# A two-layer block on one core: local attention with stationary values, the Mamba scan in PSUM, a new plan

## The chip, the cores and the metric

One Trainium2 chip, one of its cores. The metric is the device time of one execution of the whole program in microseconds (us). The engines are named as in the profile: PE is TensorE (PEld its weight loads), DVE is VectorE, ACT is ScalarE, POOL is GpSimd, SP issues most DMAs.

## What is computed

The input is 16 sequences of 256 tokens with 128 features, in fp32. Two blocks follow each other. Block 0 adds to x a Mamba layer (a scan over time with 256 inner channels and 16 states) and a layer of 8 experts of which each token takes one. Block 1 adds an attention over 16 heads with an arc-cosine kernel (called g here) and a two-layer local-attention transformer (called l here). Cut to the parts that the change touches:

```python
# Mamba: per channel d and state n, over time
h = dA * h + dBx                          # dBx = dt * B[n] * xs[d]
y = einsum('bdn,bn->bd', h, c)            # c = C[n]
y = (ys + D * xs) * silu(z)
# local attention: 8 heads of 64, windows of 64, a query sees its own window and the one before
sim = einsum('bhwid,bhwjd->bhwij', bq, bk)
sim = where(mask, -max, sim)              # mask = (i < j) | (i > j + 64)
attn = softmax(sim, axis=-1)
out = einsum('bhwij,bhwjd->bhwid', attn, bv)
x = x + out @ wo
```

## The kernel before, in words

The 16 sequences are taken as 8 pairs of 512 tokens. Everything is fp32 but the masks, which are bf16 and are added to scores by a product with a bf16 identity. Each unit of work ("m_scan", "pt", ...) has a number for the pair or layer, a stream b (which of the two sequences of a pair) and a step k. `all_units` says what each unit comes after and when it is wanted, with the offsets LATER (per kind) and STREAM (per pair). `schedule` then walks through time with the costs in STAGES, gives every engine an order and every unit its PSUM banks (8 in all), and the five programs issue their instructions in that order. The engines meet only at semaphores.

**Mamba** (units m_*). A pair has 16 steps; one step is 2 of the 16 states by one of the two halves c of 128 channels. Steps go state group by state group, both halves of each (`divmod(k, CH)`). m_ex makes dA by two Exp (ACT L1312). m_bx multiplies B by du into the SBUF tile hB (DVE L1530), m_scan scans hB in place (DVE L1536), m_hc multiplies it by C in place (DVE L1542), and m_sum adds hB up over the states by 8 transposes into a PSUM bank (PE L1013), one bank for each half, so two banks are held through the 16 steps. B and C are read from DRAM by SP, 512 KB each and broadcast over the partitions, once for each state group (L1887, L1893), two buffers of each. m_turn copies the sum out (ACT L1318) and transposes it back; m_fin finishes it on DVE.

**Local attention** (per layer, per sequence b: 32 times). heads transposes q and k. Four score units of two heads: on PE the mask (L1140, 128x128 stationary), then the second 128 queries (L1144, four tiles of 64x64) and the first 128 (L1147, two tiles of 64x128); DVE takes the negative maximum (L1684). Four pt units of two heads compute the scores again, transposed: mask (L1155), scores in three pieces for each head (L1159), then the maximum spread over the columns by two fp32 products with identities (L1165, L1166), and ACT takes Exp into the tile PT (L1426); the two buffers of PT are shared by both sequences. Eight pv units, one a head, have PT stationary and the values with a column of ones moving, 65 columns (L1179 to L1181). After three, three and two heads on takes the reciprocal of the ones' column (DVE L1694) and multiplies (DVE L1698). oT transposes the result (8 transposes of 128x128, PE L815, which is the line of all transposes but the sums') and ACT copies it out in two pieces (L1429). wo multiplies by the output weights (L1195), then come layer norm and the feed-forward part.

An fp32 product is two PE instructions in the profile (x2), a transpose is one. L1077 is the product of the g attention: values stationary in 32 columns, four heads in four groups of columns, 256 columns moving.

The lines of POOL that matter are the two additions L1823 and L1827, each of two SBUF tiles.

Of the kernel before, what the change touches and what calls it, by code (L numbers as in the profile page):

```python
# [6 lines left out]
ALU = mybir.AluOpType  # L7
# [3 lines left out]
P = 128  # L11
SEQS, L, DM = 16, 256, 128
NPAIR = SEQS // 2
T = 2 * L
# [4 lines left out]
NG = 2  # L19
# [30 lines left out]
OH = 3  # L50
OG = -(-LH // OH)
# [21 lines left out]
    "g_out": [("PE", 0.89), ("DVE", 0.68)], "out": [("DVE", 0.69), ("SP", 0.1)], "zeros": [("DVE", 0.34)],  # L73
    "shift": [("PE", 0.22), ("ACT", 0.97)], "norm": [("DVE", 0.17), ("ACT", 0.5)], "qn": [("DVE", 1.22)], "heads": [("PE", 0.88), ("ACT", 1.03)],
    "score": [("PE", 1.0), ("DVE", 0.61)], "pt": [("PE", 2.32), ("ACT", 0.7)], "pv": [("PE", 0.64)], "on": [("DVE", 0.78)],
    "oT": [("PE", 0.44), ("ACT", 0.6)], "wo": [("PE", 1.83), ("DVE", 0.42)], "ln": [("PE", 0.69), ("DVE", 0.77), ("ACT", 0.54)],
# [8 lines left out]
DUAL = ("m_du", "m_bx", "m_scan", "m_hc", "m_fin", "qn", "g_hd")  # L85
# [3 lines left out]
         "norm": "ln", "pt": "ln", "ln": "ln", "m_in": "silu", "g_tan": "tan", "gelu": "gelu"}  # L89
SWITCH = 127.0  # L90

LATER = {"down": 9, "e_down": 27, "e_lg": -177, "e_ln": 421, "e_load": -1379, "e_place": 30, "e_pre": -533, "e_route": -824,
         "e_scat": 827, "e_store": -1322, "e_tr": 261, "e_up": 40, "e_xn": -205, "e_xt": -160, "f_ln": 337, "f_tr": -1175,
         "f_xn": 125, "f_yg": 758, "g_av": 86, "g_avT": -766, "g_ev": -1332, "g_hd": -30, "g_ln": 728, "g_norm": -329, "g_oT":
         355, "g_out": 176, "g_pow": 587, "g_qkv": 73, "g_score": 51, "g_sq": 85, "g_sub": 1181, "g_tan": 60, "gelu": -398,
         "heads": 45, "hid": -32, "l_weights": 124, "ln": -103, "ln2": 5, "lnT": -6, "m_B": 636, "m_C": -449, "m_bx": 56,
         "m_dt": 27, "m_du": -6, "m_ex": -11, "m_fin": 286, "m_hc": 82, "m_in": -32, "m_load": 285, "m_out": -1531, "m_scan":
         1342, "m_sum": 17, "m_turn": -313, "m_weights": -862, "m_xp": 1631, "norm": -9, "oT": -3, "on": -102, "out": 152,
         "pt": -29, "pv": 73, "qkv": 47, "qn": -92, "score": -1, "shift": -37, "up": -72, "wo": 32, "x_load": 78, "zeros": 451}

STREAM = {("e", 0): 131, ("e", 1): 87, ("e", 2): 61, ("e", 3): 65, ("e", 4): 580, ("e", 5): 193, ("e", 6): 235,
# [13 lines left out]

LOADED = [15.0, 24.0]


BANKS = {"e_tr": 1, "e_xt": 1, "e_up": 1, "e_down": 1, "m_in": 1, "m_xp": 1, "m_dt": 1, "m_out": 1, "m_turn": 1, "f_tr": 1, "g_qkv": 1, "g_hd": 1,
         "g_score": 2, "g_avT": 1, "g_oT": 1, "g_out": 1, "shift": 1, "qkv": 1, "heads": 2, "score": 2, "pt": 2, "oT": 1, "wo": 1, "ln": 1,  # L120
         "lnT": 1, "up": 1, "down": 1}
LAYER = ("shift qkv0 qkv2 qkv3 qkv5 norm qn0 heads0 qn1 heads1 score0 score1 pt0 pt1 pv0 pv1 pv2 on0 pv3 score2 score3 "
         "pt2 pt3 pv4 pv5 on1 pv6 pv7 on2 oT0 oT1 wo ln ln2 lnT up0 up1 up2 gelu hid0 hid1 hid2 down")
LAYER = [(x.rstrip("0123456789"), int(x[-1])) if x[-1].isdigit() and x != "ln2" else (x, 0) for x in LAYER.split()]


def durations(unit):
    u, n, b, k = unit
    if u == "e_xt" and n >= GJ[1]:
# [27 lines left out]
def all_units():  # L157
# [154 lines left out]
    for b in range(2):  # L312
        unit(EARLY - 1, ("zeros", 0, b), ("f_yg", 0))
# [1690 lines left out]
```

## Time and profile before

| | |
|---|---|
| three timed runs | 2227.65, 2231.11, 2232.37 us |
| median | 2231.11 us |
| profiled execution, span | 2227.9 us |
| instructions | 37707 |
| matmul instructions | 13746 |
| mean granted TensorE clock | 0.892 of full |
| DMA | 126.74 MB, mean 57 GB/s |

The profile gives no time of its own for the profiled execution beside its span, from the first to the last instruction. The span lies within the timed runs, 3.2 us under their median. Rows of the timeline give the start and the length in us of merged instructions of one kind; the end of a matmul is modelled, so the pitch from one start to the next is the better measure of what PE spends. A granted clock of 1.00 is 2.4 GHz, 0.50 is 1.2 GHz.

### The profile page before, as it was taken

What the parts mean: (1) busy time and instruction counts of PE and PEld (TensorE: products, weight loads), DVE (VectorE), ACT (ScalarE), POOL (GpSimd) and SP (SyncE); (2) the same over time, 40 slices, a digit from 0 to 9 for tenths busy, and PEclk for the clock granted to TensorE, in tenths of its full rate; (3) what the DMA queues carried; (4) which work ended last, traced back from release to release, by engine and by line L of the source; (5) the groups of instructions that cost most, each with busy time, mean ns of one, the idle gap of its engine ahead of it and who ended that gap; (6) DMA issues with size and microseconds to landing.
All of it is one profiled execution on the core that took longest, in us unless ns stands there. A gap on an engine that the chain in (4) does not pass through costs nothing.

```text
span 2227.9 us, 37707 instructions
## 1 busy us (share of the span) xinstructions
PE 1918.6 (86%) x13746; PEld 1454.8 (65%) x13746; DVE 1749.3 (79%) x2649; ACT 1716.7 (77%) x2817; POOL 606.3 (27%) x272
## 2 busy tenths in 40 slices
PE   3677988989897889898889987899789989899997
PEld 2564766778575667667666666667666767676776
DVE  4889897675899889869976799779987898856553
ACT  2446787838887478897888989887888787897987
POOL 2351222222231033421242223403233132313221
PEclk9788888999998988999888998999889998898989
DMA  7651112442111111011200121011100111000000
GB/s 238 223 181 54 48 57 72 131 144 69 59 63 48 49 44 57 30 40 48 67 17 4 49 62 53 11 53 39 62 11 11 62 54 48 1 1 6 1 1 6
DMA packets 67687, 126.74 MB, mean 57 GB/s; under 512 B 8852, under 2 KB 40276, under 8 KB 67380
## 3 DMA queue, kind: packets, MB, share of 16 engines
q1 hardware_dynamic: 61808, 113.19, 16.2%
q0 software_dynamic: 2816, 7.21, 0.9%
q10 hardware_dynamic: 2884, 3.93, 0.5%
q8 instruction: 114, 1.87, 0.4%
q14 instruction: 65, 0.53, 0.1%
HBM read 111.46 MB, written 12.85 MB: 56 GB/s over the span
## 4 chain that ended last, share of the span: by engine, by line
PE 39%; DVE 25%; issue 17%; ACT 14%; DMA 2%; SPq 2%; POOL 0%; DVEq 0%; another core or an unknown queue 0%; ACTq 0%; POOLq 0%
PE ps L815 6%; DVE hB L1536 5%; PE ps L1063 4%; PE ps L1123 3%; DVE hB L1530 3%; PE ps L1159 2%; DVE hB L1542 2%; PE ps L1195 2%; ACT L810 2%; PE ps L1013 2%; PE ps L1166 2%; PE ps L1165 2%; DVE lss L1659 2%; DVE rb L1666 2%; ACT arena L1374 2%
## 5 line engine op out<-in xcount | busy, mean ns | idle before, releaser
L1823 POOL TENSOR_TENSOR arena<-arena 128x1024 f32<-128x1024 f32 x128 | 345.8, 2724 | 755.9 <-ACT arena L1353 755.8
L1827 POOL TENSOR_TENSOR arena<-arena,rb 128x1024 f32<-128x1024 f32 x64 | 166.2, 2596 | 672.0 <-DVE rb L1666 672.0
L1536 DVE TENSOR_TENSOR_SCAN hB<-dA,hB 128x1024 f32<-128x1024 f32 x128 | 316.7, 2479 | 0.7 <-ACT dA L1312 0.5
L815 PE MATMUL ps<-w_ident,arena 128*128 128x128 f32 x879 | 158.4, 333 | 104.9 <-DVE arena L1469 30.7
L815 PEld LDWEIGHTS ps<-w_ident,arena 128*128 128x128 f32 x879 | 127.5, 173 | 136.3 <-issue 81.2
L1374 ACT ACTIVATE arena<-arena 128x256 f32<-128x256 f32 x512 | 205.4, 402 | 2.0
L1312 ACT ACTIVATE dA<-mv,w_A_log 128x510 f32<-128x510 f32 x256 | 168.5, 712 | 49.3 <-DVE hB L1536 48.6
L1123 PE MATMUL ps<-w_l_wqkv,arena 128*128 128x512 f32 x384 | 196.3, 640 | 10.5 <-DVE nmx L1684 6.2
L810 ACT ACT_TABLE_LOAD x147 | 188.6, 1283 | 15.3 <-issue 12.7
L1530 DVE TENSOR_TENSOR hB<-BC,mv 128x1024 f32<-128x1024 f32 x128 | 189.3, 1483 | 13.8 <-PE ps L1013 10.8
L1607 DVE TENSOR_SCALAR arena<-ps 128x1024 f32<-128x1024 f32 x128 | 155.2, 1217 | 40.6 <-PE ps L1063 40.5
L1542 DVE TENSOR_TENSOR hB<-hB,BC 128x1024 f32<-128x1024 f32 x128 | 186.5, 1458 | 0.4
L1013 PE MATMUL ps<-w_ident,hB 128*128 128x128 f32 x1024 | 153.2, 298 | 34.5 <-DVE hB L1542 33.2
L1063 PE MATMUL ps<-gqT,gkT 8*128 8x256 f32 x1024 | 160.6, 460 | 21.6 <-issue 4.2
L1351 ACT ACTIVATE arena<-arena,one_b 128x2048 f32<-128x2048 f32 x64 | 127.9, 1999 | 64.3 <-DVE arena L1607 59.8
L1013 PEld LDWEIGHTS ps<-w_ident,hB 128*128 128x128 f32 x1024 | 129.6, 156 | 53.6 <-DVE hB L1542 43.9
L1426 ACT ACTIVATE PT<-ps 128x640 f32<-128x640 f32 x128 | 89.1, 696 | 73.7 <-PE ps L1166 55.8
L1684 DVE TENSOR_REDUCE nmx<-ps 128x4 f32<-128x512 f32 x128 | 87.5, 684 | 69.9 <-PE ps L1147 69.7
L1166 PE MATMUL ps<-ident_q,nmx 128*128 128x192 f32 x512 | 132.3, 341 | 0.0
L1063 PEld LDWEIGHTS ps<-gqT,gkT 8*128 8x128 f32 x1024 | 97.4, 212 | 51.3 <-issue 34.9
L1353 ACT ACTIVATE arena<-arena,one_b 128x2048 f32<-128x2048 f32 x64 | 128.2, 2003 | 2.1
L1369 ACT ACTIVATE arena<-arena,one_b 128x2048 f32<-128x2048 f32 x64 | 127.7, 1995 | 0.1
(222 smaller groups left out, 4554.6 us busy)
## 6 DMA issues: line engine op xcount, KB each, us to landing
BC<-bc_d SPq DMA_DIRECT2D x128, 512.0 KB
BC<-in_experts SPq DMA_DIRECT2D x16, 514.0 KB
arena<-in_experts SPq DMA_DIRECT2D x15, 514.0 KB
mv<-in_experts SPq DMA_DIRECT2D x15, 514.0 KB, 3.6
arena<-in_x SPq DMA_DIRECT2D x8, 256.0 KB, 5.6
xnT_d<-arena SPq DMA_DIRECT2D x8, 256.0 KB, 4.9
hB<-xnT_d SPq DMA_DIRECT2D x8, 256.0 KB
x<-in_x SPq DMA_DIRECT2D x8, 256.0 KB, 4.0
```

The lines of the kernel that those rows point to most:

```text
L810: a.preload_act_table_set(names[0])
L815: return t.transpose(out_, in_, ident[0:k, 0:k])
L1013: e = t.matmul(lb()[:, tt * P:(tt + 1) * P], hB[k % 2][:, j, tt * P:(tt + 1) * P], ident, is_transpose=True, start=q == j == tt == 0, stop ...
L1063: e = t.matmul(lb(z)[:, kt * L:(kt + 1) * L], gkT[32 * hi:32 * hi + GD, hb, kt * P:(kt + 1) * P], gqT[32 * hi:32 * hi + GD, hb], start=Tru ...
L1123: e = t.matmul(lb(z), hT1[b][:, tt * P:(tt + 1) * P], w_lqkv[:, l, (w + z) * INNER:(w + z + 1) * INNER], start=True, stop=True)
L1166: e = t.matmul(lb(z)[:, P:SC], top[1], ident_q[:], start=False, stop=True)
L1312: e = a.activation(dA[k % 2][:, j].rearrange("p (s l) -> p s l", s=2)[:, :, 1:], dtv[:, c].rearrange("p (s l) -> p s l", s=2)[:, :, 1:], A ...
L1374: e = a.activation(part, part, ACT.Exp, scale=-3.2, accum_out=vt[m % 2][:, kt, hi, GD + 2:GD + 3])
L1530: v.tensor_tensor(hB[k % 2], Bb[q % 2], bc(du[:, c:c + 1], [P, NG, T]), ALU.mult).then_inc(v_bx, 1)
L1536: v.tensor_tensor_scan(hf, flat2(dA[k % 2]), hf, 0.0, ALU.mult, ALU.add).then_inc(v_scan, 1)
L1542: v.tensor_tensor(hB[k % 2], hB[k % 2], Cb[q % 2], ALU.mult).then_inc(v_hc, 1)
L1823: g.tensor_tensor(la[m % 2][:, half], la[m % 2][:, half], cl[m % 2][:, half], ALU.subtract).then_inc(g_sub, 1)
```

## The change

1. **Attention output.** pv now has the values stationary (32 of a head's 64 features at a time) and PT moving; four heads stand in four groups of 32 PSUM partitions, as in L1077. It gives features by queries, so oT with its transposes and copies is gone. A new unit rsum multiplies PT by a column of ones spread over 32, giving each head's sums on its 32 partitions; ACT inverts them as Exp(-Ln), four heads at once; on is one DVE product per four heads. There are two of each per layer and sequence. The rows of the output weights are permuted on the host.
2. **Scores.** The masks and the first 128 queries of score use 64x64 tiles throughout. pt takes the keys in two pieces rather than three, the mask after the scores, and spreads the maximum by four transposes and two 64-column products.
3. **PT** has two buffers for each sequence.
4. **Mamba.** m_bx writes into two neighbouring PSUM banks, m_scan works there in place, m_hc reads them and writes hB. m_bx waits for the banks; the wait for the sum two steps back moves from m_bx to m_hc. From the third pair on (BY_HALF = 2) all states of one half come before the other half: one sum bank at a time, but B and C are loaded for each step, 16 of each rather than 8. The first sum is turned in the middle of the pair.
5. **Plan.** New costs, LATER and STREAM; the wait for a bank is on the unit that held it before by the plan.

```diff
-OH = 3
+OH = 4
-DUAL = ("m_du", "m_bx", "m_scan", "m_hc", "m_fin", "qn", "g_hd")
+DUAL = ("m_du", "m_bx", "m_fin", "qn", "g_hd")
+def step_of(n, k):
+    if n < BY_HALF:
+        return divmod(k, CH)
+    c, q = divmod(k, NQ)
+    return q, c
 # score, PE
-                        t.matmul(lb(z)[:, 0:SQ], ident_b[:], mask_b[:], start=True, stop=False)
+                        for y in range(2):
+                            t.matmul(lb(z)[head_rows(y), 0:SQ], ident_b[head_rows(z), head_rows(z)], mask_b[head_rows(z), y],
+                                     start=True, stop=False)
...
-                        e = t.matmul(lb(z)[:, 0:P], qT[head_rows(z), k, b * L:b * L + P], kT[head_rows(z), k, b * L:b * L + P],
-                                     start=False, stop=True)
+                            e = t.matmul(lb(z)[head_rows(y), 0:P], qT[head_rows(z), k, q0:q0 + WIN], kT[head_rows(z), k, b * L:b * L + P],
+                                         start=False, stop=True)
 # pt, PE
-                        t.matmul(lb(z)[:, 0:P], top[0], ident, start=False, stop=False)
-                        e = t.matmul(lb(z)[:, P:SC], top[1], ident_q[:], start=False, stop=True)
+                        t.matmul(lb(z)[:, 0:P], top[0], ident, is_transpose=True, start=False, stop=False)
+                        t.matmul(lb(z)[:, SC - P:SC], top[1], ident, is_transpose=True, start=False, stop=False)
+                        e = t.matmul(lb(z)[:, P:SC - P], top[1], ident[:, 0:WIN], start=False, stop=True)
+                elif u == "rsum":
...
+                            e = t.matmul(lb()[32 * hi:32 * hi + 32, at:at + cols.stop - cols.start], bc(one_b[:, 0:1], [P, 32]),
+                                         PT[b][hi // 2][:, hi % 2, cols], start=kt == 0, stop=kt == 1, skip_group_check=True)
 # pv, PE
-                    t.matmul(o0, pt[:, 0:P], vv[:, 2 * b, k], start=True, stop=True)
-                    t.matmul(o1, pt[:, P:2 * P], vv[:, 2 * b + 1, k], start=True, stop=False)
-                    t.matmul(o1, pt[:, 2 * P:], vv[:, 2 * b, k], start=False, stop=True).then_inc(p_o[b], 1)
+                    for w in range(2):
+                        for kt, cols, q0 in ((0, slice(0, SC - P), 0), (1, slice(SC - P, SC), P)):
+                            for hi in range(OH):
+                                e = t.matmul(lb()[32 * hi:32 * hi + 32, at:at + cols.stop - cols.start],
+                                             vv[:, 2 * b + kt, OH * k + hi, w * HD:(w + 1) * HD], PT[b][hi // 2][:, hi % 2, cols],
+                                             start=w == kt == 0, stop=w == kt == 1, skip_group_check=True)
 # rsum, ACT
+                    a.activation(r_, lb()[:, 0:L], ACT.Ln).then_inc(a_own, na.up())
+                    a.activation(r_, r_, ACT.Exp, scale=-1.0).then_inc(a_rs[b], 1)
 # on, DVE
-                    v.reciprocal(r_, o_[:, :, :, LD]).then_inc(v_own, nv.up())
-                    v.tensor_tensor(oo[b].rearrange("p t (h e) -> p t h e", e=LD)[:, :, h0:h0 + m], o_[:, :, :, 0:LD],
+                    v.tensor_tensor(o_, bank(("pv", i, b, k)).rearrange("p (w t) -> p w t", w=2), bc(oT[b][:, 2 * k + 1:2 * k + 2], [P, 2, L]), ALU.mult).then_inc(v_oT[b], 1)
 # m_bx, m_scan, m_hc, DVE
-                    if m >= 2:
-                        v.wait_ge(p_ys, m - 1)
+                    for z in range(2):
+                        into(unit, z, v)
-                    v.tensor_tensor(hB[k % 2], Bb[q % 2], bc(du[:, c:c + 1], [P, NG, T]), ALU.mult).then_inc(v_bx, 1)
+                    v.tensor_tensor(two_banks(unit), Bb[j % 2], bc(du[:, c:c + 1], [P, NG, T]), ALU.mult).then_inc(v_bx, 1)
-                    v.tensor_tensor_scan(hf, flat2(dA[k % 2]), hf, 0.0, ALU.mult, ALU.add).then_inc(v_scan, 1)
+                    v.tensor_tensor_scan(h_, flat2(dA[k % 2]), h_, 0.0, ALU.mult, ALU.add).then_inc(v_scan, 1)
+                    if m >= 2:
+                        v.wait_ge(p_ys, m - 1)
-                    v.tensor_tensor(hB[k % 2], hB[k % 2], Cb[q % 2], ALU.mult).then_inc(v_hc, 1)
+                    v.tensor_tensor(hB[k % 2], two_banks(("m_bx", i, b, k)), Cb[j % 2], ALU.mult).then_inc(v_hc, 1)
```

## Rows read from the trace of the kernel before

**Rows 1.** The page, part 1: busy us, share of the span, instructions.
```profile
PE 1918.6 (86%) x13746; PEld 1454.8 (65%) x13746; DVE 1749.3 (79%) x2649; ACT 1716.7 (77%) x2817; POOL 606.3 (27%) x272
```

**Rows 2.** Windows: length, busy us of PE, PEld, DVE, ACT, POOL, clock, DMA, GB/s.
```profile
0.00:100.00 100.00, 48.85 (x217) 37.86 (x217) 65.63 (x191) 34.83 (x78) 23.25 (x30) 0.81 0.69 225
500.00:700.00 200.00, 176.56 (x1317) 134.25 (x1318) 161.07 (x235) 167.81 (x270) 52.58 (x25) 0.93 0.21 65
1300.00:1500.00 200.00, 173.59 (x1267) 127.86 (x1266) 167.81 (x242) 179.45 (x300) 55.13 (x22) 0.91 0.13 41
```

**Rows 3.** The chain that ended last, share of the span by engine.
```profile
PE 39%; DVE 25%; issue 17%; ACT 14%; DMA 2%; SPq 2%; POOL 0%; DVEq 0%; another core or an unknown queue 0%; ACTq 0%; POOLq 0%
```

**Rows 4.** Timeline of PE, about 645 to 653 us: start, us, line.
```profile
645.78 0.45 PE L1155 MATMUL ps<-maskT_b,ident_b 128*128 128x320 bf16 x2 [0.58 <-DVE nmx L1684]
...
646.97 0.49 PE L1165 MATMUL ps<-w_ident,nmx 128*128 128x128 f32 x2
...
648.17 1.04 PE L1013 MATMUL ps<-w_ident,hB 128*128 128x128 f32 x8
649.59 1.07 PE L1077 MATMUL ps<-arena,vt 128*32 128x256 f32 x16 [0.38 <-issue]
650.59 0.39 PE L1140 MATMUL ps<-mask_b,ident_b 128*128 128x256 bf16 x2
650.91 0.45 PE L1144 MATMUL ps<-arena 64*64 64x128 f32 x8
651.29 0.49 PE L1147 MATMUL ps<-arena 64*128 64x128 f32 x4
651.72 0.66 PE L815 MATMUL ps<-w_ident,avS 128*128 128x128 f32 x4
652.21 1.04 PE L1013 MATMUL ps<-w_ident,hB 128*128 128x128 f32 x8
```

**Rows 5.** The same view, two heads of pv in a row, about 2150 us.
```profile
2149.82 0.33 PE L1179 MATMUL ps<-arena,PT 128*128 128x65 f32 x2
...
2150.44 0.39 PE L1179 MATMUL ps<-arena,PT 128*128 128x65 f32 x2
```

**Rows 6.** DVE groups by line: count, busy us, mean ns, idle before.
```profile
L1536 DVE TENSOR_TENSOR_SCAN hB<-dA,hB 128x1024 f32<-128x1024 f32 x128 | 316.7, 2479 | 0.7 <-ACT dA L1312 0.5
L1542 DVE TENSOR_TENSOR hB<-hB,BC 128x1024 f32<-128x1024 f32 x128 | 186.5, 1458 | 0.4
L1661 DVE TENSOR_TENSOR arena<-ps,w_rot 128x1024 f32<-128x1024 f32 x64 | 78.4, 1225 | 2.2
```

**Rows 7.** DVE lines one by one: count, then least, median and greatest ns.
```profile
L1536 DVE TENSOR_TENSOR_SCAN hB<-dA,hB x128: 2258/2284/4464, 64.5 to 1926.2; 128x1024 f32<-128x1024 f32 x128
L1698 DVE TENSOR_TENSOR arena<-ps,rs x96: 424/557/559, 232.5 to 2204.8; 128x384 f32<-128x384 f32 x64, 128x256 f32<-128x256 f32 x32
L1694 DVE RECIPROCAL rs<-ps x96: 152/185/198, 232.2 to 2204.6; 128x6 f32<-128x6 f32 x64, 128x4 f32<-128x4 f32 x32
L1644 DVE TENSOR_TENSOR go<-ps,x x8: 658/682/692, 564.9 to 2222.9; 128x512 f32<-128x512 f32 x8
```

**Rows 8.** ACT groups by line, columns as in rows 6.
```profile
L1429 ACT ACTIVATE arena<-ps 128x512 f32<-128x512 f32 x64 | 36.4, 592 | 24.6 <-PE ps L815 24.3
L1441 ACT ACTIVATE arena<-ps,w_l_b 128x256 f32<-128x256 f32 x64 | 27.0, 470 | 4.7 <-PE ps L1218 4.3
L1374 ACT ACTIVATE arena<-arena 128x256 f32<-128x256 f32 x512 | 205.4, 402 | 2.0
```

**Rows 9.** Windows as in rows 2, for the clock and the DMA rate.
```profile
645.70:648.20 2.50, 2.42 (x23) 2.07 (x24) 2.50 (x3) 1.65 (x3) 0.00 (x0) 1.00 0.64 205
2165.00:2171.00 6.00, 5.59 (x32) 5.18 (x36) 2.83 (x10) 4.00 (x14) 0.00 (x0) 0.53 0.00 0
```

**Rows 10.** Timeline of PE, what fills the second window of rows 9.
```profile
2165.41 5.38 PE L815 MATMUL ps<-w_ident,arena 128*128 128x128 f32 x24 [0.74 <-DVE arena L1676]
```

**Rows 11.** Waits: who waited for whom, us in total, times, longest.
```profile
DVE hB L1530 <- PE ps L1013: 10.8, 11, 3.7
```

More of the change, by code:

```diff
@@ L90 @@
 SWITCH = 127.0
[L92 to L99, printed above, removed]
@@ L101 @@
-STREAM = {("e", 0): 131, ("e", 1): 87, ("e", 2): 61, ("e", 3): 65, ("e", 4): 580, ("e", 5): 193, ("e", 6): 235,
[13 rows of a table removed]
+LATER = {"down": 17.13, "e_down": 0.92, "e_lg": -1373.3, "e_ln": 621.99, "e_load": -1698.97, "e_place": -129.783, "e_pre": 351.489,
+         "e_route": 144.702, "e_scat": 829.618, "e_store": -223.789, "e_tr": -184.595, "e_up": 44.242, "e_xn": -28.591, "e_xt": -830.714,
+         "f_ln": 818.98, "f_tr": -1660.36, "f_xn": -118.536, "f_yg": -111.816, "g_av": 89.144, "g_avT": -202.085, "g_ev": -784.392,
+         "g_hd": -35.958, "g_ln": 938.103, "g_norm": -59.145, "g_oT": 238.89, "g_out": 718.35, "g_pow": 876.48, "g_qkv": 45.815,
+         "g_score": 49.652, "g_sq": 72.566, "g_sub": 570.978, "g_tan": 44.449, "gelu": -343.785, "heads": 43.677, "hid": -127.469,
+         "l_weights": 625.975, "ln": -124.928, "ln2": 1.634, "lnT": -15.963, "m_B": -153.424, "m_C": 17.261, "m_bx": 50.752,
+         "m_dt": 18.917, "m_du": 21.175, "m_ex": -16.259, "m_fin": 74.245, "m_hc": 137.244, "m_in": -23.847, "m_load": -295.604,
+         "m_out": -935.123, "m_scan": 731.575, "m_sum": 14.942, "m_turn": -247.837, "m_weights": -173.243, "m_xp": 895.808,
+         "norm": -15.561, "on": -140.182, "out": 284.565, "pt": -39.622, "pv": 82.873, "qkv": 47.209, "qn": -65.566, "rsum": -2.347,
+         "score": -4.24, "shift": -70.641, "up": -71.786, "wo": 25.239, "x_load": 44.744}
@@ L127, in durations, with loads_in @@
+def loads_in(n, j):
+    return (sum(loads_of(x) for x in range(n)) + j) // 2 + 1
 def durations(unit):
@@ L276, in all_units @@
                     elif u == "qkv":
-                        x = [("shift", n, b)] + [("down", n - 1, b) for z in range(1) if n] + [("pv", n - 1, b, 7) for z in range(1) if n and k % 3 == 2]
+                        x = [("shift", n, b)] + [("down", n - 1, b) for z in range(1) if n] + [("pv", n - 1, b, OG - 1) for z in range(1) if n and k % 3 == 2]
                     elif u == "norm":
@@ L361, in frees_banks @@
         return (0, ("y", n, k))
+    if u == "m_hc":
+        return (-1, ("m_bx", n, b, k))
     if u == "m_fin":
@@ L365, in frees_banks @@
         return (-1, ("av", n, b, k))
+    if u == "rsum":
+        return (-1, unit)
     if u == "on":
-        return (-1, ("o", n, b, k))
+        return (-1, ("pv", n, b, k))
     if u == "ln2":
@@ L375, in frees_banks @@
         return (-1, ("up", n, b, k))
-    if u in BANKS and u not in ("ln", "up"):
+    if u in BANKS and u not in ("ln", "up", "m_bx"):
         return (-1, unit)
@@ L386, in holds @@
         takes[2], frees[3] = ["rb"], ["rb"]
-    if u == "pt":
-        takes[1] = [f"PT{k % 2}"]
-    if u == "pv" and k % 2:
-        frees[0] = [f"PT{k // 2 % 2}"]
     return takes, frees
@@ L405, in schedule @@
     plan = {e: [] for e in engines}
-    idle, banks = list(range(8)), {}
+    idle, banks, held_by, before_it = list(range(8)), {}, {}, {}
     taken = set()
@@ L510, in schedule @@
             finish(x[2], x[3], x[0])
-    plan["banks"] = banks
+    plan["banks"], plan["before"] = banks, before_it
     return plan
@@ L521, in shared_before @@
     table = {}
-    slot, rb = [(0, 0), (0, 0)], (0, 0)
-    for unit in order(plan, "ACT"):
-        u, n, b, k = unit
-        if u == "pt":
-            table[unit] = slot[k % 2]
-            slot[k % 2] = (b, LH * n + 2 * k + 2)
+    rb = (0, 0)
     for unit in order(plan, "DVE"):
@@ L793, in build, with into @@
         done_with = {}
-        def into(unit, m=0):
-            number = plan["banks"][bank_of(unit)][m]
-            if number in done_with:
-                t.wait_ge(*done_with[number])
+        def into(unit, m=0, engine=t):
+            held = plan["before"][bank_of(unit), m]
+            if held and held[0][0] == "m_bx":
+                engine.wait_ge(v_hc, STEPS * held[0][1] + held[0][3] + 1)
+            elif held:
+                engine.wait_ge(*done_with[held])
         def read_by(unit, semaphore, value, m=0):
-            done_with[plan["banks"][bank_of(unit)][m]] = (semaphore, value)
+            done_with[bank_of(unit), m] = (semaphore, value)
         table = [None]
@@ L1986, in constants @@
     q0 = np.arange(P)[None]
-    for name, ahead in (("mask", (m0, m1)), ("maskT", (q0 - i, q0 - i, q0[:, 0:WIN] + P - i))):
-        d_ = np.concatenate(ahead, 1)
+    rows = np.concatenate([np.arange(WIN), np.arange(WIN)])
+    scores = np.concatenate([m0, m1], 1)
+    mask = np.concatenate([scores[rows], scores[rows + WIN]], 1)
+    for name, d_ in (("mask", mask), ("maskT", np.concatenate([np.arange(SC - P)[None] - i, q0 - i], 1))):
         r[name] = np.where((d_ < 0) | (d_ > WIN), np.float32(NEG), np.float32(0)).astype(np.float32)
```

231 lines of the change are left out of this document (116 added, 115 removed), and 27 rows, old and new, of the table STREAM.

## The prediction

> **What bounds the kernel now.** I read the page's busy shares first, then windows, the chain, the timeline of PE and single lines. PE is busy 1919 us of 2228, DVE 1749, ACT 1717 [rows 1]: no engine is a wall, and three are near one. Seen by stretch it is tighter: from 500 to 700 us PE is busy 88% and from 1300 to 1500 us it is ACT with 90% [rows 2]. Only the first 100 us are loose on all engines. The chain that ended last is 39% PE, 25% DVE, 14% ACT, 17% issue [rows 3]. So this is a list of many small units of which the busiest engine changes, PE most often. Work taken from PE pays most, but in part, as the next engine stands 170 us behind. An effect under 0.2% (4 us) can't be told from none here.
>
> **Score, on PE.** A unit takes 1.13 us at full clock: mask 0.32, then 0.38 and 0.43 [rows 4], from the start of L1140 to that of L815. L1144 is 8 instructions of 128 columns in four tiles. At the 0.12 us a 128-column pass that the 4 transposes behind it show (0.49), two rounds of four are 0.24; the rest of its 0.38, 0.14, I take as the price of changing tiles. After: 0.24 twice, the mask as one round of 256 bf16 columns, about 0.11, and one change: 0.73. Saved 0.40 x 128 = 51 us. Bounds: 0.10 if tiles don't overlap better than now, 0.50 at best.
>
> **pt, on PE.** A unit is 2.39 us: mask and scores 1.19, spreading the maximum 1.20 [rows 4], by the starts of L1155, L1165 and L1013. The spreading becomes 4 transposes (0.49) and two 64-column products. A head of pv is three products of 65 columns in 0.62 [rows 5], 0.21 each, so 0.42: together 0.91, saved 0.29. Scores: four of 12 instructions go and their columns are appended to others. Between 0 (columns unchanged) and 0.4 (four short passes at 0.1); I take 0.2, near the middle, as a short pass costs more than its columns. Saved 0.49 x 128 = 63 us.
>
> **pv, rsum and oT, on PE.** Removed: 256 heads x 0.62 = 159 us and 64 x 0.49 = 31 us of transposes. Added: L1077 does the same kind of product, 16 instructions of 256 columns in four groups, in 1.00 us [rows 4]. A pv is 32 instructions of 160 columns on average, 5120 against 4096: 1.25. A rsum is half: 0.63. 64 x 1.88 = 120. Saved 70 us. If the groups ran one after another it would be four times the 120, but L1077's own 1.00 for what is 16 full passes excludes this.
>
> Sum on PE: 51 + 63 + 70 = 184 us at full clock, bounds 110 and 240. At the mean granted clock of 0.892 that is 206 us of its time: 1919 to 1713.
>
> **ACT.** 64 copies of 0.592 go; 64 times a Ln from PSUM, priced by L1441 of the same size (0.470), and an Exp from SBUF as L1374 (0.402) come [rows 8]: 55.8 - 37.9 = +18 us, 1735 in all. Both need the table that pt's Exp has loaded. Table loads may go up or down with the plan; I leave them. ACT becomes the busiest engine.
>
> **DVE.** on: 96 reciprocals of 0.185 and 64 x 0.557 + 32 x 0.424 go, 67 us; 64 products from PSUM at 0.682 come, 44: -23 us [rows 7]. The scan has a median of 2284 and a mean of 2479 ns [rows 6, 7], so (2479 - 2284) x 128 = 25 us are held up by POOL's additions. m_hc, 1458 against 1225 for L1661, which has the same shape but reads PSUM and is hardly ever disturbed [rows 6], gives 30 us more. Both now read one tile from SBUF only, like L1661. m_bx still reads two, and the POOL addition that was delayed by a scan may now meet it; I take 40 of the 55 us, bounds 10 and 55. Reading PSUM costs nothing visible: L1661 is at 1225. Writing PSUM from DVE is in no row; nearest is reading it, so I take 0, bounds -0.05 and +0.1 us for each of 256 writes, -13 to +26 us. DVE: 1749 - 63 = 1686.
>
> By the Trainium skill (VectorE: DVE Perf Modes, the section on the TRN2 errata) a VectorE instruction with PSUM as its source has a fixed part of 120 cycles against 58, about 65 ns more. By it the scan and m_hc would lose 17 us. The 1225 ns of L1661 doesn't bear that out here.
>
> **Mamba's order and DMAs.** From the third pair on SP issues 16 + 16 loads a pair rather than 8 + 8: 96 more of 512 KB. At 205 GB/s [rows 9] a load is 2.6 us, two of them 5.1 us a step. Two buffers leave a load the scans, m_hc and the other m_bx of two steps, over 8 us when steps run close (1.22 + 2.28 + 1.22 each), and DMA is at 10 to 20% of its engines there [rows 2]. I cost them at nothing. If the cover fails, it is up to 5.1 - 4.7 = 0.4 us for each of 96 steps, 38 us; what waits is m_bx, and behind it all of DVE. On SP's queue the loads wait for DVE; behind them stand x_load, m_load and out, wanted late. m_bx no longer waits for the sum two steps back, only 10.8 us now [rows 11]; m_hc takes that wait, later in the step, where it is rarer. The first turn of a pair in its middle spreads work and shortens the pair's end: no price.
>
> **Banks.** The scan's pair of banks is held at least 4.7 us a step, 128 x 4.7 x 2 = 1200 bank-us of 8 x 2228; the second sum bank that goes from the third pair on frees a like amount. I cost it at nothing; see the rivals.
>
> **The sum.** Three readings. (a) The load of the three engines goes from 5385 to 1713 + 1686 + 1735 = 5134, -4.7%; at the same mean share the span is 2124. (b) The busiest engine at PE's present 86% gives 1735 / 0.86 = 2017. (c) By the chain: PE's 869 us shrink like its work, 206/1919, by 93; DVE's 557 by 63/1749, 20; issue, 379 us, much of it PE between its instructions, by about 15: 2100. I take (c): 2100 us of span. The plan is new as well; its effect has no row, and I take none. With the 3 us between span and median: **2103 us**.
>
> **The rivals.**
> - ACT takes over. It gets 18 us more, and its two-instruction inverse stands between rsum and on, on its in-order queue. For it: ACT is at 90% in [rows 2]. Against: its load elsewhere is lower, and the units can move. If its share goes only from 77% to 80%, the time is 1735 / 0.80 = 2169. Chance 0.14.
> - The clock falls. For it: in the second window of [rows 9] PE is busy 5.59 of 6 us, all but a little of it with 24 transposes [rows 10], at a granted clock of 0.53, and their pitch is 0.22 us instead of 0.12. The change makes transposes of products and takes dense work away. The full-clock work after, 1919 x 0.892 - 184 = 1528 us, takes 1713 us at 0.892 and 1798 at 0.85; half of the 85 on the chain gives 2103 + 43 = 2146. Against: oT's transposes go too, and the columns of pv remain. Chance 0.10. The Trainium skill (TensorE: Matmul & The Clock Gate, Part 4) says that transpose mode does not count as busy for the clock as other products do; by that rule the trace agrees with [rows 10], and this case would be the likely one.
> - It packs better. PT no longer shared, DVE undisturbed, PE with air: reading (b), 2020. Chance 0.10.
> - Slower: **m_bx's banks**. It needs two neighbouring free banks, and DVE's queue is in order: while it waits for the reader of what lay there (ACT's pt copy, a clamp, a layer norm), scans, clamps and maxima behind it stand still, and ACT and PE with them. It decides from 128 us / 128 steps = 1.0 us of wait a step on the chain; at 1.3 us it is 2103 + 166 = 2269. Against: the planner counts banks, and those freed match. Chance 0.08.
>
> **How the numbers follow.** The forecast of about 2103 us has 0.58. The range reaches from the better packing, 2015, to a little above the ACT case, 2190; it takes in PE's bounds (184 between 110 and 240 us moves the chain by about 35 us each way) and the loads' 38. Left out are the bank case and a part of each end. Faster by over 0.2%: 0.58 + 0.14 + 0.10 + 0.10, less the corner where small losses add up, 0.03, which is "same": 0.89. Slower: 0.08.
>
> **What the profile after should show.** PE near 1700 us busy; L1698's successor 64 times at 0.68; score pitch 0.7 and pt 1.9 at full clock; pv 1.25 and rsum 0.65; mean of scan and m_hc near their medians; ACT about 1735 with two new groups of 64; B and C loads 224 with no wait of m_bx for a DMA; clock at 0.87 or above. I am wrong if scans in PSUM take longer than 2.35 us, if m_bx waits for banks over 60 us in all, or if ACT's idle time grows where PE's shrinks.

## The result: no faster, slower by 0.9%

The changed kernel takes 2251.6 us, the kernel before 2232.3, medians of seven runs each: the ratio is 1.009, with a 95% interval from 1.006 to 1.012. Forecast were 2103 us, 5.8% less, in a range from 2015 to 2190. The profiled execution took 2262.57 us, its span 2261.3.

Nearly every price of a unit's work was right, and the time went the other way. The profile after, part 1 of the page, beside [rows 1]:

```profile
span 2261.3 us, 40539 instructions
...
PE 1788.6 (79%) x15282; PEld 1293.3 (57%) x15282; DVE 1697.8 (75%) x2517; ACT 1739.7 (77%) x2887; POOL 541.0 (24%) x270
```

PE lost 130 us of busy time, DVE 51 us, ACT gained 23 us (18 priced; the Ln and Exp in place of the copies came to 15, and six more table loads to 8). All three engines idle more: PE 473 us instead of 309, DVE 564 instead of 479, ACT 522 instead of 511. The same windows as [rows 2]:

```profile
0.00:100.00 100.00, 49.75 (x226) 39.24 (x227) 63.91 (x187) 35.85 (x83) 16.60 (x25) 0.82 0.67 227
...
500.00:700.00 200.00, 163.96 (x1413) 117.18 (x1411) 162.17 (x204) 164.79 (x267) 50.72 (x26) 0.86 0.29 94
...
1300.00:1500.00 200.00, 163.21 (x1374) 113.05 (x1374) 156.73 (x230) 177.77 (x300) 48.39 (x22) 0.85 0.21 68
```

In both later stretches PE is busy for less time and its clock is lower (0.86 for 0.93, 0.85 for 0.91). These stretches don't single one out. The last scan of Mamba starts at 1910.7 us, 16 us earlier than before (1926.2, [rows 7]), and from there to the end the changed kernel takes 351 us instead of 302, so it is what stands behind Mamba that ends late. The mean granted clock is 0.863, before 0.892.

The units on PE, from its timeline (start, length, line). Each sits in a stretch with a granted clock of 1.00:

```profile
1010.34 0.36 PE L1224 MATMUL ps<-arena 128*32 128x192 f32 x2
...
1011.56 0.66 PE L849 MATMUL ps<-w_ident,go 128*128 128x128 f32 x4
...
1043.86 0.36 PE L1212 MATMUL ps<-arena,one_b 128*32 128x192 f32 x2
...
1044.54 0.30 PE L1171 MATMUL ps<-mask_b,ident_b 64*64 64x256 bf16 x4
1044.68 0.39 PE L1176 MATMUL ps<-arena 64*64 64x128 f32 x8
1044.89 0.39 PE L1181 MATMUL ps<-arena 64*64 64x128 f32 x8
1045.21 0.98 PE L1043 MATMUL ps<-w_ident,hB 128*128 128x128 f32 x7
...
1339.04 0.82 PE L1192 MATMUL ps<-arena 64*128 64x192 f32 x8
1339.79 0.45 PE L1195 MATMUL ps<-maskT_b,ident_b 128*128 128x320 bf16 x2
1340.07 0.27 PE L1200 MATMUL ps<-w_ident,nmx 128*128 128x128 f32 x1
...
1340.85 0.61 PE L849 MATMUL ps<-w_ident,avS 128*128 128x128 f32 x4
```

From the start of a unit to that of what follows, pv takes 1.22 us (priced 1.25), rsum 0.68 (0.63), a score 0.14 + 0.21 + 0.32 = 0.67 (0.73; before 1.13), pt 1.81 (1.90) and of it the maximum 0.78 (0.91). Four heads in four column groups do overlap: at the 0.12 us for 128 columns of [rows 4], the 32 passes of pv, 160 columns on average, would take 4.8 us one after another.

The lines of DVE, count and least, median and greatest ns, beside [rows 7]:

```profile
L1573 DVE TENSOR_TENSOR ps<-BC,mv x128: 1207/1230/3409, 62.4 to 1908.4; 128x1024 f32<-128x1024 f32 x128
...
L1579 DVE TENSOR_TENSOR_SCAN ps<-dA,ps x128: 2261/2285/2296, 64.7 to 1910.7; 128x1024 f32<-128x1024 f32 x128
...
L1587 DVE TENSOR_TENSOR hB<-ps,BC x128: 1194/1214/1226, 68.0 to 1914.0; 128x1024 f32<-128x1024 f32 x128
...
L1644 DVE TENSOR_TENSOR gpad<-gqk,gpad x64: 259/284/7380, 202.9 to 2117.7; 128x128 f32<-128x128 f32 x64
```

The scan never takes more than 2296 ns where it had gone up to 4464, and m_hc never more than 1226: with one SBUF input neither shows a long execution any more. Writing PSUM costs m_bx 12 ns by the median (1230 against the 1218 that the same line showed in SBUF). But some of the collisions have only moved. L1644, two SBUF inputs, now takes up to 7.4 us, and two groups have grown (busy us, mean ns, idle before):

```profile
L1721 DVE TENSOR_TENSOR arena<-arena,lss 128x1024 f32<-128x1024 f32 x64 | 95.5, 1522 | 5.0 <-ACT lss L1450 4.6
...
L1644 DVE TENSOR_TENSOR gpad<-gqk,gpad 128x128 f32<-128x128 f32 x64 | 41.4, 647 | 9.1 <-ACT gpad L1373 7.1 <-PE ps L849 1.9
```

The kernel before had 77.6 and 23.7 us there, so 36 of the 58 us that the scan and m_hc gained came back. The rest of DVE's 51 us is the cheaper on (44 us for 67).

ACT's new groups, beside [rows 8]: the Ln from PSUM took 380 ns, under the 470 assumed, the Exp 417.

```profile
L1472 ACT ACTIVATE arena<-arena 128x256 f32<-128x256 f32 x64 | 26.7, 417 | 2.0
L1470 ACT ACTIVATE arena<-ps 128x256 f32<-128x256 f32 x64 | 24.3, 380 | 24.2 <-PE ps L1212 23.4
```

What grew are waits between engines. First a line of the kernel before, then of the one after (who waited for whom, us in total, times, longest):

```profile
DVE nmx L1684 <- PE ps L1147: 69.7, 48, 5.3
```

```profile
DVE nmx L1729 <- PE ps L1181: 97.2, 58, 6.1
...
ACT arena L1439 <- PE ps L1153: 55.5, 30, 6.3
...
DVE vt L1661 <- ACT arena L1413: 44.1, 20, 6.5
```

The score unit takes 0.67 us on PE where it took 1.13, and DVE waits for it longer. The likely reading is that it waits for the unit's turn in PE's order. m_bx waits 12.9 us in all, of it 1.1 for a load: neither the banks nor the loads stop it where the profile can see. (The chain of the changed kernel could be followed back through 15% of the span only, so it isn't compared with [rows 3].)

### The profile page after: what moved, and what is told of

Read it like the earlier page. It is cut to its first block and busy times, and to the rows that moved or that the text cites. A ratio compares the mean times of both kernels' runs of the same rounds, so it can differ in the third digit from the quotient of the medians.

```text
span 2261.3 us, 40539 instructions
## 1 busy us (share of the span) xinstructions
PE 1788.6 (79%) x15282; PEld 1293.3 (57%) x15282; DVE 1697.8 (75%) x2517; ACT 1739.7 (77%) x2887; POOL 541.0 (24%) x270
## 5 line engine op out<-in xcount | busy, mean ns | idle before, releaser
L1855 POOL TENSOR_TENSOR arena<-arena 128x1024 f32<-128x1024 f32 x128 | 316.3, 2493 | 622.8 <-ACT arena L1392 622.6
L1579 DVE TENSOR_TENSOR_SCAN ps<-dA,ps 128x1024 f32<-128x1024 f32 x128 | 291.0, 2284 | 1.6 <-ACT dA L1351 1.0
L1573 DVE TENSOR_TENSOR ps<-BC,mv 128x1024 f32<-128x1024 f32 x128 | 181.6, 1425 | 12.9 <-ACT arena L1457 4.1
L849 PE MATMUL ps<-w_ident,arena 128*128 128x128 f32 x623 | 112.1, 326 | 99.5 <-DVE arena L1512 28.6
L849 PEld LDWEIGHTS ps<-w_ident,arena 128*128 128x128 f32 x623 | 87.2, 169 | 125.0 <-issue 83.2
L1587 DVE TENSOR_TENSOR hB<-ps,BC 128x1024 f32<-128x1024 f32 x128 | 154.4, 1214 | 4.4 <-PE ps L1043 3.6
L1192 PE MATMUL ps<-arena 64*128 64x192 f32 (+1 forms) x1024 | 118.5, 352 | 35.1 <-DVE rb L1711 13.9
L1390 ACT ACTIVATE arena<-arena,one_b 128x2048 f32<-128x2048 f32 x64 | 127.7, 1996 | 22.8 <-DVE arena L1652 20.9
L1192 PEld LDWEIGHTS ps<-arena 64*128 64x128 f32 x1024 | 92.5, 207 | 83.8 <-issue 49.9
L1153 PEld LDWEIGHTS ps<-w_l_wqkv,arena 128*128 128x128 f32 x384 | 74.4, 211 | 101.9 <-issue 94.1
L1392 ACT ACTIVATE arena<-arena,one_b 128x2048 f32<-128x2048 f32 x64 | 128.2, 2003 | 2.1
```

Source lines behind the costliest of these rows:

```text
L849: return t.transpose(out_, in_, ident[0:k, 0:k])
L1153: e = t.matmul(lb(z), hT1[b][:, tt * P:(tt + 1) * P], w_lqkv[:, l, (w + z) * INNER:(w + z + 1) * INNER], start=True, stop=True)
L1192: t.matmul(lb(z)[:, cols], kT[head_rows(z), k, at:at + P], qT[head_rows(z), k, at:at + cols.stop - cols.start], start=kt == 0, stop=False)
L1573: v.tensor_tensor(two_banks(unit), Bb[j % 2], bc(du[:, c:c + 1], [P, NG, T]), ALU.mult).then_inc(v_bx, 1)
L1579: v.tensor_tensor_scan(h_, flat2(dA[k % 2]), h_, 0.0, ALU.mult, ALU.add).then_inc(v_scan, 1)
L1855: g.tensor_tensor(la[m % 2][:, half], la[m % 2][:, half], cl[m % 2][:, half], ALU.subtract).then_inc(g_sub, 1)
```

## The experiments

Two theories stood at first. **Order**: the work was saved, but the kernel before had an order fitted to it very closely, and the new offsets fit the new units less well. **Clock**: the change takes streaming work from PE, its granted clock falls, and this eats the gain. A third, **structure**, is that a part of the change brings waits of its own.

The runs were taken in several rounds, each with the kernel before beside it, whose median went from 2230 to 2239 us. The ratios below are to the kernel before of the same round; a difference between runs of different rounds is taken from them.

### r1: the change with a better order

The kernel's own schedule ends at a time that it works out when it is built. An offset or two at a time was moved at random, steps by which this end came earlier were kept, and a worse step now and then, less and less often; some 6500 steps.

```diff
-LATER = {"down": 17.13, "e_down": 0.92, ...}
+LATER = {(numbers found by the search)}
-STREAM = {("-", 0): 147.932, ...}
+STREAM = {(numbers found by the search)}
```

> The changed kernel with other numbers in LATER and STREAM, found by trying small random steps and keeping those by which the kernel's own schedule ends earlier (it puts the end at 2193 us; 2248 for the change, 2233 for the kernel before). All instructions are the same in kind and number but table loads; only their order and their banks differ. Theory order (the saved work is there, the new order doesn't pack it): 2180 to 2215 us, faster than both, with busy times of PE, DVE and ACT within 15 us of the change's. Rival clock (the granted clock fell to 0.863 as the work changed, and that eats the gain): no order mends it, 2235 to 2265 us. Rival structure (the new waits for banks, for rsum and for more loads are what costs): 2235 or more as well.

Measured: 2219.5 us, 0.994 of before (0.992 to 0.995), faster than both. PE 1761, DVE 1701, ACT 1731 us busy, with PE 28 us under the change's, nearly twice the 15 expected; clock 0.872. Some 32 us of the change's time is its order. The clock takes part in this: PE's work at full clock, as busy time by mean clock, is nearly the same (1535 us, in the change 1544), and 18 of the 28 us are what 1789 us lose by going from 0.863 to 0.872. The time stops short of the 2215 expected, and of its schedule's 2193. The same search on the kernel before, 6500 steps from its own offsets, found next to nothing (its schedule's end went from 2232.9 to 2232.3): by this measure that one was at its best already.

### r2 and r3: both kernels with offsets shaken alike

```diff
-LATER = {"down": 9, "e_down": 27, ...}
+LATER = {(each number plus a normal deviate of 10 us)}
```

> The kernel before with each number of LATER moved at random (normal, 10 us, the middle one of 15 such draws by the schedule's own end). Same instructions, another order. Theory order: the kernel before owes much of its time to numbers that fit it closely, so 2330 to 2370 us, 5% slower. Rivals clock and structure say nothing of this; if order mattered little it would be within 1% of 2232 us.

> The changed kernel with the same treatment as r2 (middle one of 15 draws). Theory order: the change's numbers fit it less closely, so it loses little, 2255 to 2285 us, and stands 3 to 4% under r2: that difference is what the change is worth when neither order is fitted. Rival structure: it is no faster than r2.

Measured: 2351.8 us for the kernel before, 1.053 (1.051 to 1.054), and 2280.8 for the changed one, 1.021 (1.019 to 1.023). A shake of 10 us costs the kernel before 5.3% and the change 1.2% (1.021 against 1.009). Shaken alike, the change is faster by 1 - 2280.8 / 2351.8 = 3.0%, 71 us. Both as the order theory had it. It is one draw of each, the middle one of 15 by the schedule's end; the spread of others was not run. Here too order and clock go together: in r2 PE does the same work at full clock as before (1968.8 x 0.871 = 1715 us, before 1711), but at 0.871 for 0.892, and so is busy 50 us longer.

### r4: cheaper PE work in the old order

```diff
-                        t.matmul(lb(z)[:, 0:P], top[0], ident, start=False, stop=False)
-                        e = t.matmul(lb(z)[:, P:SC], top[1], ident_q[:], start=False, stop=True)
+                        t.matmul(lb(z)[:, 0:P], top[0], ident, is_transpose=True, start=False, stop=False)
+                        t.matmul(lb(z)[:, P:2 * P], top[1], ident, is_transpose=True, start=False, stop=False)
+                        e = t.matmul(lb(z)[:, 2 * P:SC], top[1], ident[:, 0:WIN], start=False, stop=True)
```

and score's masks and first queries as in the change.

> The kernel before in its own order, with only the cheaper PE bodies of score (64x64 tiles for the masks and the first queries) and of pt's maximum (four transposes and two 64-column products in place of four fp32 products); mask table, identity copy and nothing else differ. By the prediction's prices PE loses 51 + 37 = 88 us of full-clock work, 97 at 0.9. Theory order: an order made for dearer units gives back little, 2205 to 2225 us, and PE's idle time grows by over 60 us. If PE's work were the bound (the prediction's reading of the chain, 45% of it): 2190 us or less. Rival clock: the granted clock falls under 0.88 and the time stays at 2230.

Measured: 2237.3 us, the median of ten runs, 1.002 (1.001 to 1.004). Nothing was gained. The page:

```profile
span 2227.4 us, 39241 instructions
...
PE 1867.1 (84%) x14514; PEld 1427.0 (64%) x14514; DVE 1752.5 (79%) x2647; ACT 1715.4 (77%) x2817; POOL 607.6 (27%) x272
```

The clock is 0.874 in this execution, the fastest of the ten. Busy time by mean clock went from 1918.6 x 0.892 = 1711 to 1867.1 x 0.874 = 1632, so 79 us of full-clock work are gone, near the 88 priced; of these PE's busy time shows 51, and the span none. This is the clock rival's result on both counts (under 0.88, and the time stays). The order theory's 2205 to 2225 us was missed, and PE's idle time grew by 51 us, not by over 60. The ten runs of this one kernel go the same way: the two at a clock of 0.873 and 0.874 took 2229 us, the eight at 0.864 to 0.869 took 2233 to 2244. By themselves they don't say which of the two sets the other; r8 and r11 bear on that.

### r7 and r8: more and less work for PE, order kept

r7 is the change with products in place of its transposes, r8 the kernel before almost without the spreading of the maximum.

```diff
 # r7, from the changed kernel
-                        t.matmul(lb(z)[:, 0:P], top[0], ident, is_transpose=True, start=False, stop=False)
-                        t.matmul(lb(z)[:, SC - P:SC], top[1], ident, is_transpose=True, start=False, stop=False)
+                        t.matmul(lb(z)[:, 0:P], top[0], ident, start=False, stop=False)
+                        t.matmul(lb(z)[:, SC - P:SC], top[1], ident, start=False, stop=False)
 # r8, from the kernel before
-                        t.matmul(lb(z)[:, 0:P], top[0], ident, start=False, stop=False)
-                        e = t.matmul(lb(z)[:, P:SC], top[1], ident_q[:], start=False, stop=True)
+                        e = t.matmul(lb(z)[:, P:P + 1], top[1], ident_q[:, 0:1], start=False, stop=True)
```

> The changed kernel in its own order, where the maximum is spread by fp32 products (two instructions of 128 columns each) where the change uses transposes: 512 transposes become 1024 passes. PE gets 512 x 0.11 = 55 us more of full-clock work. Theory order (PE is not what sets the end in this order): within 0.5% of the change's 2252 us, and the clock rises from 0.863 to about 0.875. If transposes had cost the change its clock and the clock its time (rival clock): faster than 2240 us. If PE's work is the bound: 2275 or more.

> The kernel before in its own order, with the spreading of the maximum left out but for one column a head (its Exp isn't scaled by the maximum, so the result isn't the reference's): four fp32 products of 128 and 192 columns become two of one column. PE loses some 0.9 us x 128 = 115 us of full-clock work. Theory order: 2205 to 2235 us, as r4; the clock falls to 0.86 or less and PE idles more. If PE's work sets the end: 2150 us or less.

Measured: r7 2278.0 us, 1.018 (1.014 to 1.022). PE's full-clock work rises by 1823.8 x 0.877 - 1788.6 x 0.863 = 56 us, as priced, and the clock to 0.877, as expected. The time rises by 26 us as measured and by 21 by the ratios (1.018 for 1.009). That is outside the order theory's 0.5% and refutes the clock rival as it was put here: PE's work does lie on the path, by somewhat under half, and these 512 transposes are not what costs the change its time, though they cost it clock.

r8 is 2268.1 us, 1.014 (1.010 to 1.019): **slower** with less to do. The windows from 500 to 2100 us (busy us of PE, PEld, DVE, ACT, POOL, clock, DMA), first of the kernel before, then of r8:

```profile
500.00:2100.00 1600.00, 1420.74 (x10405) 1069.14 (x10406) 1301.28 (x1837) 1317.63 (x2126) 435.02 (x174) 0.91 0.12 39
```

```profile
500.00:2100.00 1600.00, 1401.61 (x9795) 1038.86 (x9794) 1289.29 (x1819) 1300.39 (x2102) 428.29 (x171) 0.85 0.12 40
```

PE has 1915.8 us busy in all, as many as before, for 1915.8 x 0.851 = 1630 us of full-clock work instead of 1711 (81 us less; 115 were priced). All that was saved went into a lower clock, and more. The unchanged instructions show it one by one. The group of the sums (L1013), before and in r8 (busy us, mean ns of one, idle before):

```profile
L1013 PE MATMUL ps<-w_ident,hB 128*128 128x128 f32 x1024 | 153.2, 298 | 34.5 <-DVE hB L1542 33.2 <-DVE nmx L1684 1.2
```

```profile
L1013 PE MATMUL ps<-w_ident,hB 128*128 128x128 f32 x1024 | 164.4, 313 | 34.3 <-DVE hB L1541 32.3 <-DVE nmx L1683 1.9
```

Added over all groups of PE but the spreading and pt's mask, these busy times come to 2036 us before and 2131 in r8 (the groups overlap, so the sum is more than PE's busy time): the same instructions take 95 us longer. DVE (1744 us for 1749) and ACT (1718 for 1717) don't. The order and the waits are the same in both, so a shorter unit by itself can make nothing start later; what got longer is PE's instructions. None of the expectations had this; r11 was made for it.

### r11: idle PE filled again

```diff
-                        t.matmul(lb(z)[:, 0:SC], ident_b[:], maskT_b[:], start=True, stop=False)
+                        for again in range(3):
+                            t.matmul(lb(z)[:, 0:SC], ident_b[:], maskT_b[:], start=True, stop=again < 2)
```

> r8 with idle PE filled again: the bf16 mask product of each pt unit is run three times instead of once, the first two overwritten (128x128, 320 columns), ahead of the wait for the maximum. That adds 2 x 2 x 0.13 us x 128 = 68 us of full-clock work to PE. Rival clock (r8 is slower than before as the clock fell from 0.892 to 0.851, since what was taken away had kept the array streaming): the clock rises over 0.865 and the time falls below r8's 2268 us although PE does more. Theory order, with PE's work half on the path as r7 showed (26 us for 55): slower than r8, 2285 to 2310 us.

Measured: 2248.7 us, 1.007 (1.0054 to 1.0095) of before, against r8's 1.014 (1.0098 to 1.0188): the intervals only just don't meet, and half of what r8 lost is back. PE does 1938.9 x 0.872 = 1691 us of full-clock work, 60 more than r8, and the median is lower. The profiled executions don't show the gain in time, as they are r8's fastest and r11's slowest (spans of 2253.6 and 2253.8 us); they show the clock. The same window, and the group of the sums:

```profile
500.00:2100.00 1600.00, 1419.27 (x10175) 1049.38 (x10174) 1293.98 (x1811) 1294.81 (x2099) 423.47 (x170) 0.88 0.12 39
```

```profile
L1013 PE MATMUL ps<-w_ident,hB 128*128 128x128 f32 x1024 | 158.9, 305 | 37.0 <-DVE hB L1542 35.0 <-DVE nmx L1684 1.3 <-DVE arena L1607 0.5
```

This is the clock rival's result on both counts: here a lighter PE made the kernel slower, and added work that computes nothing made it faster. The other half of r8's loss fits as well: the groups that came to 2036 us before and 2131 in r8 come to 2084 here, so half of their lengthening is left too. It is not a rule for any added work: in r7, where PE had 56 us more to do and the clock also rose, the time rose. The Trainium skill (TensorE: Matmul & The Clock Gate, Part 1) says that the throttled state is the default and that activity releases it; the granted clocks of before, r8 and r11, 0.892, 0.851 and 0.872, agree in direction.

### r5, r6, r9, r10: the parts, each with a searched order

All four had a search of about the length of r1's, so that the orders are on the same footing, as far as one search of each can give it. r5 is the new attention with Mamba as before, r9 adds half-by-half order and its 224 loads, r10 has the scan in PSUM but states first, r6 is the new Mamba with the old attention.

```diff
 # r5, from the changed kernel (r9: the same with BY_HALF = 2)
-BY_HALF = 2
+BY_HALF = 8
-                    v.tensor_tensor(two_banks(unit), Bb[j % 2], bc(du[:, c:c + 1], [P, NG, T]), ALU.mult).then_inc(v_bx, 1)
+                    v.tensor_tensor(hB[k % 2], Bb[j % 2], bc(du[:, c:c + 1], [P, NG, T]), ALU.mult).then_inc(v_bx, 1)
...
-                    h_ = flat2(two_banks(("m_bx", i, b, k)))
+                    h_ = flat2(hB[k % 2])
...
 # r10, from the changed kernel
-BY_HALF = 2
+BY_HALF = 8
```

> The changed kernel's attention (stationary values, rsum, cheaper scores, PT of its own for each sequence) with Mamba as it was before: scan in SBUF, two sum banks, 128 loads of B and C rather than 224. Its offsets were searched for as long as those of r1 (its own schedule ends at 2200 us). If the gain of r1 comes from the attention: 2205 to 2235 us, within 0.7% of r1, with PE's busy time as in r1. If the Mamba part is what costs in the change (loads, banks for m_bx): clearly faster than r1, under 2205. If the Mamba part carries the gain: 2240 or more.

> The other half: the kernel before with the changed Mamba alone (scan in PSUM, half by half, 224 loads), the old attention, offsets searched for as long as r1's (its schedule ends at 2308 us). If undisturbed scans on DVE (about 55 us by the prediction) were worth much, 2235 us or less. If banks bind, as the scan's pair and the old attention's banks compete: 2300 to 2330 us, with DVE's scan and m_hc at their medians (2284 and 1214 ns) all the same.

> r5 (new attention, scan in SBUF) with the half-by-half order and its 224 loads from the third pair on, offsets searched as long as r1's and r5's (its own schedule ends at 2193 us, r5's at 2200). If the 96 added loads and SP's longer queue are what makes r1 20 us slower than r5: 2215 us or more. If the scan in PSUM is (its banks): within 0.5% of r5's 2199 us.

> The changed kernel with the scan in PSUM but states first throughout (BY_HALF = 8): 128 loads, two sum banks and the scan's two banks held together, offsets searched as long (its schedule ends at 2233 us). If banks are the price of the scan in PSUM: 2225 to 2250 us, slower than r9 and r5 by over 1%, though the scans are undisturbed. If banks are free here: 2200 or less.

Measured, with the end of the kernel's own schedule beside it:

```
                                scan   order            loads  schedule  chip us   ratio (95%)
r5  new attention               SBUF   states first       128      2200   2198.5   0.981 (0.977 to 0.985)
r9  new attention               SBUF   half by half       224      2193   2200.1   0.986 (0.983 to 0.988)
r1  the change, searched        PSUM   half by half       224      2193   2219.5   0.994 (0.992 to 0.995)
r10 new attention               PSUM   states first       128      2233   2239.7   1.003 (1.001 to 1.005)
r6  old attention               PSUM   half by half       224      2308   2318.4   1.035 (1.031 to 1.040)
```

Each time fell in the range that one of the readings had given. The gain is the attention's: r5 is 1.9% under before. The 96 added loads cost nothing that shows (r9 against r5; no wait of m_bx for a load stands in r9's list of waits), though by the ratios, whose intervals overlap, up to 10 us are not excluded. The scan in PSUM costs 0.8%, 18 us, half by half (r1 against r9) and 2.2%, 49 us, states first (r10 against r5), and with the old attention the whole new Mamba is 3.5% slower than before. Its good side is there too: DVE has 1701 us busy in r1 and 1732 in r5.

```profile
PE 1761.5 (80%) x15282; PEld 1276.3 (58%) x15282; DVE 1732.1 (79%) x2517; ACT 1733.2 (79%) x2883; POOL 599.2 (27%) x270
```

That is r5's page, part 1. DVE does 31 us more than in r1, and the kernel is 21 us faster (28 by the ratios). In r10 m_bx itself hardly waits, 14.3 us in all, against 13.3 in r5. Its longest waits for readers of its banks (us in total, times, longest):

```profile
DVE ps L1550 <- ACT PT L1442: 3.3, 3, 1.9
DVE ps L1550 <- ACT arena L1434: 3.1, 3, 1.7
```

So the price isn't paid as a wait of m_bx. Two of eight banks are kept from others while a scan is on, four with both sums. States first, this may act through the schedule, which then ends at 2233 us rather than 2200. Half by half it can't be told so: r1's and r9's schedules end at the same 2193 us, and the chip is 18 us apart. What these two schedules differ in is DVE, with 1747 us of work in r1's and 1806 in r9's, 59 us less for the scan in PSUM; on the chip DVE has 28 us less (1701 and 1729). So the schedule may credit the scan in PSUM with more than it gives, the collisions that move to other lines among it. Banks as the reason are argued, from r10 costing more than r1, and not shown; a version with the same order and only the tile moved would settle it and was not run.

### r12: the fastest

```diff
 # from r5: LATER and STREAM alone, searched for three times as long again
```

> r5 with its offsets searched three times as long again (its own schedule ends at 2186 us, r5's at 2200). Theory order: the schedule's gain carries over in part, 2180 to 2198 us, the fastest of all here. If r5 is at the floor of its busy times on this chip (PE 1762, DVE 1732, ACT 1733): 2199 us again, within 0.2%.

Measured: 2193.8 us, 0.982 (0.978 to 0.985), the lowest median of all; its ratio is that of r5, so whether the longer search gave anything on the chip stays open. Both beat both kernels, as r1 and r9 do.

## Why the prediction was wrong

By its steps:

- **Prices on PE**: right. Priced at full clock were 184 us less; the page gives 1711 - 1788.6 x 0.863 = 168. The single units differ from their prices by 0.09 us at most, and by their pitches 202 us are saved (59 for score, 74 for pt, 69 for the rest); busy time by mean clock is a rough product.
- **ACT +18**: +23. **DVE -63**: -51; the scan and m_hc gained 58 us, all of the 55 that could be had, and 36 came back on L1721 and L1644. Writing PSUM was rightly put near nothing (12 ns). The clause "the POOL addition that was delayed by a scan may now meet it" named m_bx, but it was two other lines.
- **Loads and banks at nothing**: the loads cost nothing that shows (r9). The scan in PSUM does: 18 us. The forecast had a rival in "m_bx's banks", but put it as a wait in front of m_bx, which is 12.9 us in all. Whether the banks are the price, and where it is paid, stays open.
- **"At the mean granted clock of 0.892"**: this term was wrong. PE's time was worked out at a clock that the saved work itself had kept up. With 168 us less of full-clock work it was 0.863, and of the 206 us expected PE's busy time shows 130. In the old order r4 and r8 give back everything. The clock rival had a chance of 0.10 and a price of 43 us, though the same paragraph says that by the rule on transposes it would be the likely case; by r8 the price can be more than the gain, and the mechanism there is less work, not transposes.
- **"(c) By the chain: PE's 869 us shrink like its work ... DVE's 557"**: the step that failed most by size. It takes PE's gain off the chain and leaves the parts of the other engines nearly as they are. r5 has the new attention in a searched order; its chain, of a span of 2203.6 us, is

```profile
PE 31%; DVE 28%; ACT 18%; issue 18%; DMA 2%; SPq 2%; POOL 0%; DVEq 0%; ACTq 0%; POOLq 0%
```

  Against [rows 3], and as near as whole per cents allow, PE's part has fallen by some 186 us (39% to 31%), even more than the 93 forecast, but DVE's has grown by 60, ACT's by 85 and that of issue by 18, though DVE is not busier than before and ACT by 17 us only. What PE gives up, the others take over. In r5, r9 and r12 PE is busy 157 to 178 us less than before, and the time is 31 to 42 us less: about 0.2 to 0.27 us for one of PE, where the sum took 0.45 and a part of issue.
- **"The plan is new as well; its effect has no row, and I take none"**: the step that turned the sign. The order before was worth 5.3% to its kernel (r2), the change's own was worth 1.2% to it (r3), and a search gave it 32 us (r1). Shaken alike the parts give 3.0%, about half of the 5.8% forecast; searched orders give 1.9% for the attention alone and 0.6% with the Mamba part.
- **The three readings** of the sum agreed with each other as all three scale the same busy times, and so did not check each other.
- **The signs**: "clock at 0.87 or above" and "PE near 1700" failed (0.863 and 1789). None of the three signs under "I am wrong if" came: scans in PSUM take 2.285 us, m_bx waits 12.9 us, and ACT's idle time grew by 11 us while PE's grew by 163 instead of shrinking.

The 19 us of loss are, by these runs: the parts in a searched order would have been 13 us to the good of before (r1, 0.994), and the order left some 32 us. Of the 148 us between forecast and result 32 are the order (r1) and 18 the scan in PSUM (r9). The other 98 are the sum over the chain and the clock in it; no run parts these two.

## What to carry to other kernels

Where a kernel's order comes from a planner with fitted numbers, a change to its units undoes the fit; give both kernels the same amount of fitting, or shake both alike, before a part is judged, and look at the end that the planner itself works out, which came within 1.3% of the chip in all ten kernels whose order was made for them here. When three engines are near each other, don't leave the chain's other parts as they are when one shrinks; here they took over most of it. Price PE's work at the clock that will be left after the change: in this kernel, with PE close to the others, work taken off a fixed order came back whole as a lower clock. And change one thing at a time: the attention was worth 1.9%, and the Mamba part gave two thirds of it away (r1), the scan's move to PSUM alone took all of it where states come first (r10).

## What the runs showed of the hardware

- Less PE work can make a kernel slower: r8 against before, 81 us of full-clock work less, 1.4% more time, clock 0.851 for 0.892, with the same instructions 95 us longer by the sum of their groups; 60 us of overwritten products put back gave half of that back (r11, 1.007 for 1.014, and 2084 us of these groups for 2131).
- A scan of 1024 fp32 elements in place in PSUM takes 2285 ns by the median, in SBUF 2284. m_bx into PSUM takes 1230 for 1218.
- Ln of 256 columns from PSUM takes 380 ns (no bias tile), where the Gelu of the same size, which also reads a bias from the tile w_l_b, takes 470; no run parts the function from the bias.
- Sixteen fp32 passes in four groups of 32 columns, 192 and 128 columns long, take 0.68 us, and 32 take 1.22. At the 0.12 us for 128 columns of [rows 4] they would take 2.4 and 4.8 us in turn, so about four run side by side.
- What a PSUM scan frees on DVE comes back in part elsewhere: the scan and m_hc gained 58 us, and two other lines with two SBUF inputs lost 36 (the changed kernel against the one before).
